# Gated cross-attention with a top-2 expert layer on one core: the prologue reordered, constant rows filled by two engines, weight loads in pairs, tiles aligned to 64 bytes

## The reference

```python
# attention: q from layernorm(x), k and v from ctx; 16 heads of 8
scores = einsum('bhqd,bhkd->bhqk', Q, K) / sqrt(8) + mask + window   # |i-j|<=32 or a global token (<16)
x = x + tanh(g_xattn) * (softmax(scores) @ V @ wo + bo)
# 8 experts, the best 2 for each token, F = 512
h = layernorm(x)
w, idx = top_k(softmax(h @ gate_w), 2); w = w / w.sum()
x = x + tanh(g_ffn) * sum_i w_i * (silu(h @ w1[i]) * (h @ w3[i])) @ w2[i]
```

## Time and profile before

| | us |
|---|---|
| median of 3 runs | 486.2 |
| lowest, highest | 484.93, 486.38 |
| profiled execution: span from the first to the last instruction | 458.1 |
| PE busy in the span | 407.4 (89%) |
| DVE, POOL, ACT busy | 290.9, 259.4, 239.6 |

### The profile page before, as it was taken

One profiled execution on the slowest core, in us unless ns is written; L12 is line 12 of the kernel. 1 busy time (PEld: TensorE's weight loads), 2 busy tenths in 40 slices (PEclk: granted clock), 3 DMA queues, 4 the chain that ended last, 5 costly groups with the idle time before them and its releaser, 6 DMA issues.

```text
span 458.1 us, 14422 instructions
## 1 busy us (share of the span) xinstructions
PE 407.4 (89%) x4547; PEld 360.1 (79%) x4548; DVE 290.9 (64%) x786; ACT 239.6 (52%) x564; POOL 259.4 (57%) x312
## 2 busy tenths in 40 slices
PE   2879979999999998997879899988999999999970
PEld 1647658877777776776669799888999999999960
DVE  3876798887888887889546368544444554554420
ACT  2758506667677675766666534233444444444430
POOL 5743554334654737473646568776666665655560
PEclk9989979999999999999999999999999999999995
DMA  7964557457766666485223233334444343333235
GB/s 215 279 123 94 96 96 185 90 105 113 170 147 136 152 134 161 106 216 169 65 69 75 45 52 48 54 67 61 69 70 58 44 54 46 46 47 40 24 29 189
DMA packets 74783, 46.24 MB, mean 101 GB/s; under 512 B 8608, under 2 KB 71490, under 8 KB 74562
## 3 DMA queue, kind: packets, MB, share of 16 engines
q1 hardware_dynamic: 59072, 34.84, 33.2%
q0 software_dynamic: 12272, 8.92, 14.9%
q10 hardware_dynamic: 3392, 1.88, 1.7%
HBM read 18.12 MB, written 14.20 MB: 71 GB/s over the span
## 4 chain that ended last, share of the span: by engine, by line
PE 62%; DMA 9%; issue 7%; DVE 6%; ACT 6%; POOL 4%; ACTq 2%; POOLq 1%; DVEq 0%
PE ps_scores L1612 20%; PE ps_max_scores L1620 10%; DMA sums_scratch<-yt,xg 8%; PE ps_values L897 7%; PE ps_max_scores L853 6%; PE ps_scores L883 5%; PE ps_scores L837 3%; PE ps_max_scores L837 2%; POOL expert_rows_scratch L1328 2%; PE ps_out L921 1%; ACT xn L474 1%; DVE rsplit L1119 1%; ACT w_all L464 1%; DVE qkf L558 1%; POOL sums_scratch L1733 1%
## 5 line engine op out<-in xcount | busy, mean ns | idle before, releaser
L1733 POOL DMA_INDIRECT sums_scratch<-yt,xg x71 | 115.9, 1633 | 66.9 <-DMA sums_scratch<-yt,xg 28.1
L1612 PE MATMUL ps_scores<-xgT,qs 128*128 128x128 f32 x1136 | 141.1, 278 | 5.1 <-ACT xgT L1658 3.8
L1612 PEld LDWEIGHTS ps_scores<-xgT,qs 128*128 128x128 f32 x1136 | 134.1, 194 | 7.1 <-ACT xgT L1658 4.5
L1699 DVE TENSOR_TENSOR qs<-qs,ps_scores 128x512 f32<-128x512 f32 x71 | 48.8, 688 | 88.4 <-PE ps_scores L1612 70.5
L1119 DVE TENSOR_REDUCE rsplit<-ps_max_scores 128x4 f32<-128x512 f32 x128 | 84.8, 685 | 15.0 <-PE ps_max_scores L837 11.2
L1328 POOL DMA_INDIRECT expert_rows_scratch<-xr,pos x64 | 66.4, 1037 | 25.6 <-issue 13.1
L1620 PE MATMUL ps_max_scores<-w_all,qs 128*128 x568 | 75.6, 276 | 2.8 <-ACT yt L1669 2.3
L1620 PEld LDWEIGHTS ps_max_scores<-w_all,qs 128*128 128x128 f32 x568 | 69.0, 192 | 3.8 <-issue 3.6
L1027 ACT ACTIVATE pT<-ps_scores 128x1024 f32<-128x1024 f32 x64 | 62.0, 1022 | 18.1 <-PE ps_scores L837 17.8
L1662 ACT ACTIVATE qs<-ps_scores 128x512 f32<-128x512 f32 x71 | 42.3, 596 | 30.3 <-PE ps_scores L1612 30.3
L1669 ACT ACTIVATE yt<-ps_max_scores,xg 128x128 f32<-128x128 f32 x71 | 26.1, 368 | 60.4 <-PE ps_max_scores L1620 40.4
(11 more groups left out here) (202 smaller groups left out, 527.8 us busy)
## 6 DMA issues: line engine op xcount, KB each, us to landing
qs<-w_all SPq DMA_DIRECT2D x96, 64.0 KB
ks<-w_all SPq DMA_DIRECT2D x96, 64.0 KB
w_all<-in_L_ffn_w_dram SPq DMA_DIRECT2D x24, 256.0 KB
xg<-expert_rows_scratch SPq DMA_DIRECT2D x71, 65.0 KB, 1.9
xs<-in_x_dram SPq DMA_DIRECT2D x4, 512.0 KB, 5.6
sums_scratch<-xs SPq DMA_DIRECT2D x8, 256.0 KB, 4.5
sums_scratch<-yt,xg POOLq DMA_INDIRECT x71, 3.3
expert_rows_scratch<-fill SPq DMA_DIRECT2D x16, 65.0 KB, 2.5
```

Source lines behind the costliest of these rows:

```text
L1612: ins = nc.tensor.matmul(bank[u % 2][:, c * P:(c + 1) * P], w13[:, u % 2, n, c * P:(c + 1) * P], xgT[:], start=True, stop=True)
L1699: nc.vector.tensor_tensor(hidT[:, u % 2], act_s[:, u % 2], ps_b[u % 2], ALU.mult).then_inc(hid_ready, 1)
L1733: pool.indirect_dma_start(out=z_d, out_offset=bass.IndirectOffsetOnAxis(ap=xg_u[:, u, X_IDX:X_IDX + 1], axis=0), in_=yt[:, u % YRING], in_ ...
```

## The change

- **Loads.** x comes in five chunks of 1, 1, 2, 2, 2 groups instead of four of two. `wo`, `bo`, `gate_w`, the mask, `bv` and the two gates are issued by SP instead of ACT, `wo` and the mask ahead of `fixed`. The biases have a semaphore of their own, so that the projection waits for three weights only.
- **ACT.** A one-element square root is executed right behind the weights' DMAs, which moves the load of its table there. Copy and normalise of the first groups change places; `std` 3 stands behind `copy_turned(3)`, `std` 4 behind `first_part(2)`.
- **PE.** Group 0 is projected before the router's four matmuls and group 1's turn; the turns of groups 1 and 2 stand between a group's q/k and v matmuls.
- **DVE.** Statistics of the last two chunks move behind `split` of groups 1 and 2.
- **Constant rows.** DVE fills `qs0`, POOL fills `ks0` in one instruction each; `qs1` and `ks1` are filled by DVE in four halves, one for each of groups 2 to 5 (`fix_second`). The 11 copies by SP are gone. The halves of group 1 wait for all four fills.
- **Weights.** No block of six; behind each half from group 2 on up to two pieces go, in order, of experts below the group's number.
- **Alignment.** Tiles whose size is an odd multiple of 32 bytes get 32 bytes of padding behind them.

```diff
+LINE = 64
         def sb(name, shape, dt=F32):
-            return stack.enter_context(nc.sbuf_tensor(name, shape, dt))
+            tile = stack.enter_context(nc.sbuf_tensor(name, shape, dt))
+            used = int(np.prod(shape[1:])) * (2 if dt == BF16 else 4)
+            if -used % LINE >= LINE // 2:
+                stack.enter_context(nc.sbuf_tensor(f"{name}_rest", [P, LINE // 8], F32))
+            return tile
...
-        XCH = 4
+        CHUNKS = (GB, GB, 2 * GB, 2 * GB, 2 * GB)
...
             load_x(0)
             load_ctx(0)
+            load_x(1)
             load_ctx(1)
-            load_x(1)
+            load_x(2)
+            sp.dma_start(mrow[:], mask_in).then_inc(mask_loaded, 16)
+            sp.dma_start(wo_x[:, 0:D], wo).then_inc(router_loaded, 16)
...
-            for side, (tile, rows) in enumerate(((qs, STAY_ROWS[0]), (ks, STAY_ROWS[1] + ((ROWS_M, ROWS_X),)))):
-                sp.wait_ge(fixed_ready, side + 1)
-                for lo, hi in rows:
-                    sp.dma_start(tile[1][lo:hi], tile[0][lo:hi]).then_inc(tile_copied, 16)
-
+            sp.wait_ge(fixed_ready, 1)
+            sp.wait_ge(keys_fixed, 1)
             sp.wait_ge(mpart_stored, 16)
             for g in range(2):
                 sp.wait_ge(parts_ready, g + 1)
                 if g == 1:
-                    sp.wait_ge(tile_copied, 16 * TILE_COPIES)
+                    sp.wait_ge(second_fixed, FIXES)
...
+        def fixed_rows(side, u, heads):
+
+            to = (qs, ks)[side][u][0:ROWS_X, heads].rearrange("p h (b s) -> p (h b) s", s=S)
+            return to, fixed[0:ROWS_X, side].unsqueeze(1).to_broadcast([ROWS_X, to.shape[1], S])
...
+            pool.wait_ge(fixed_loaded, 16 * 4)
+            keys, rows = fixed_rows(1, 0, slice(0, H))
+            pool.tensor_copy(keys, rows).then_inc(keys_fixed, 1)
...
+            last_part(0)
             pool.memset(wmask[:], 0.0).then_inc(pool_step, 1)
...
+            def fix_second(n):
+
+                nc.vector.tensor_copy(*fixed_rows(n // 2, 1, slice(n % 2 * (H // 2), (n % 2 + 1) * (H // 2))))\
+                    .then_inc(second_fixed, 1)
...
             for g in range(NG - 2):
                 split(g, g % 2)
                 bias_v(g)
-                if g < 2:
+                take_gates(g)
+                if 0 < g < 3:
+                    statistics(g + 2)
                     invert(g + 2)
-                if g == 0:
-                    statistics(3)
-                take_gates(g)
+                if g >= 2:
+                    fix_second(g - 2)
...
-            for e in range(2):
-                for n in range(3):
-                    load_weights(e, n)
+            pieces = [(e, n) for e in range(E) for n in range(3)]
             for g in range(2, NG):
...
-                    if g >= 3:
-                        for n in (range(0, 1), range(1, 3))[p]:
-                            load_weights(g - 1, n)
+                    for piece in range(2):
+                        if pieces[0][0] < g:
+                            load_weights(*pieces.pop(0))
```

More of the change, by code:

```diff
@@ L188, in build, with chunk, chunk_of @@
         idx_f = sb("idx_f", [P, 2, GB])
-        XCH = 4
-        x_loaded = [sem(f"x_loaded{i}") for i in range(XCH)]
+        CHUNKS = (GB, GB, 2 * GB, 2 * GB, 2 * GB)
+        assert sum(CHUNKS) == B
+        def chunk(i):
+            return slice(sum(CHUNKS[:i]), sum(CHUNKS[:i + 1]))
+        def chunk_of(g):
+            return 0 if g == 0 else 1 + g // 2
+        x_loaded = [sem(f"x_loaded{i}") for i in range(len(CHUNKS))]
         proj_loaded = sem("proj_loaded")
+        bias_loaded = sem("bias_loaded")
         by_dim_ready = sem("by_dim_ready")
@@ L509, in statistics @@
             def statistics(i):
-                n = B // XCH
+                at = range(B)[chunk(i)]
                 dve.wait_ge(x_loaded[i], 16)
-                for b in range(i * n, (i + 1) * n):
+                for b in at:
                     nc.vector.bn_stats(stats[:, b], xs[:, b]).then_inc(var_stats, 1)
-                dve.wait_ge(var_stats, (2 * i + 1) * n)
-                for b in range(i * n, (i + 1) * n):
+                dve.wait_ge(var_stats, at.start + at.stop)
+                for b in at:
@@ L586, in project_tensor, with turn @@
         def project_tensor(pe):
-            def turn(g, u, between=None):
+            def turn(g, u):
                 if not (isinstance(g, int) and g == 0):
@@ L636, in project_tensor, with second @@
             pe.wait_ge(ident_ready, 2)
-            turn(0, 0, turn_router)
-            turn(1, 1)
+            turn(0, 0)
             pe.wait_ge(proj_loaded, 16 * PROJ)
             pe.wait_ge(by_dim_ready, 2)
-            for g in range(NG - 2):
+            def second():
+                turn_router()
+                turn(1, 1)
+            project(0, 0, second)
+            project_gates(0, 0)
+            project(1, 1, lambda: turn(2, 0))
+            project_gates(1, 1)
+            turn(3, 1)
+            for g in range(2, NG - 2):
                 project(g, g % 2)
```

123 lines of the change are left out of this document (63 added, 60 removed).

## The result

| us | before | changed |
|---|---|---|
| median of 4 runs | 485.63 | 513.69 |
| lowest, highest | 484.93, 486.38 | 510.87, 515.93 |
| profiled execution: its own time | not given | 515.93 |
| its span | 458.1 | 514.2 |

The ratio is 1.0596, with a 95% interval of 1.0526 to 1.0665: 28.1 us more, where 13.3 were forecast and 505 was the end of the range.

What follows compares the result with a forecast made beforehand. PE's own work was taken to bound attention and experts, leaving only the prologue loose. Terms 3.7 + 0.3 + 5.7 + 3.6 = 13.3 us gave span 471.4 and, with 28.1 around it, 499.5 us; range 486.5 to 505.

Steps and rivals of the forecast that it cites:

- The start: Prologue: projection starts between 9.5 and 11, but POOL's copy holds DVE's `shift` until 23.4; group 1 ends 3.7 us later.
- Group 1 to 2: Prologue round between the ends of these groups' first parts: 9.3 us against 8.97 before, so +0.3.
- Group 2 to 3: Prologue: ACT waits for the last chunk's statistics, put behind group 2's split; 10.85 us against 5.17, so +5.7.
- Groups 3 to 6: Prologue: DVE's fills wait for POOL's third part, rounds become 5.6 us; split of group 6 17.0 us behind, +3.6.
- first softmax scores at 81.0: Start of attention: PE's first softmax scores move from 67.69 to 81.0, by the summed 13.3 us.
- Padding changes no count and no shape ... so I give it zero: Tile alignment: `w_all` reads run in the experts' window with PE full, so padding was put at zero.
- The rest of the span, 390.4 us, follows unchanged: Attention and experts: PE's own work is the bound, so everything after the first softmax scores keeps its length.
- PE waited on the halves of group 1: Attention: named as a sign of being wrong; forecast had these halves in place by 85, wanted at 86 and 96.
- The 28.1 us around the span, taken as fixed: Outside the profiled span: 28.1 us added to span 471.4 to give 499.5, assuming the profile was of a median run.
- At nothing: SP's queue: removing the 11 copies (15.8 us of queue) and splitting the block of six weight loads change nothing.
- the rivals: Four alternatives: POOL's copy not holding DVE (0.15), ACT setting the pace (0.15), no change (0.06), Slower still (0.07).
- Slower still: Rival, prologue: POOL copies at its two-input rate, 17.0 us; 8.3 us more, 507.8 in all; chance 0.07.

Runs made afterwards that it cites:

- after_scores_256_again: Repeat of after_scores_256 (changed kernel, padding kept, spacer putting score tiles on a multiple of 256 bytes) in the fifth session: 473.43 us, 1.0295 of the kernel before.
- after_old_layout: Changed kernel with every tile at its address of before (no padding, new small tile behind the others): 501.49 us, no ratio given.
- fifth session: Last session of experiments: changed kernel word for word (480.52 us) beside it with score tiles on a multiple of 256 bytes (473.43); kernel before 459.9.
- 485 session: A session in which the unchanged kernel before had a median near 485 us: 484.7 in the second, 486.4 in the third; the head's times (485.6) belong to one.
- 460 session: A session in which the unchanged kernel before had a median near 460 us: 460.1, 460.2 and 459.9 in the first, fourth and fifth.
- after_old_weights: Changed kernel with the weight loads in the order of before (block of six behind group 1's halves): 478.57 us, 1.0392 of the kernel before.
- after_fourth: Changed kernel word for word, timed again in the fifth session: 480.52 us, 1.0433 of the kernel before.
- after_scores_256: Changed kernel with its padding and a 128-byte spacer putting the score tiles on a multiple of 256 bytes again: 471.91 us, 1.0266 of the kernel before.
- before_scores_128: Kernel before with a 128-byte spacer ahead of the score tiles, which begin 128 bytes past a multiple of 256: 463.9 us, 1.007 of the kernel before.
- after_third: Changed kernel word for word, timed and profiled in the third session: 509.12 us, 1.0446 of the kernel before.
- before_third: Kernel before, word for word, timed and profiled again in the third session: 487.94 us, ratio 1.0039.

## Why the prediction was wrong

Step by step, in the prediction's own terms (the changed kernel's profile against the one of before):

- **The start**: projection at 11.08, forecast 9.5 to 11. Near enough. `shift` of the third chunk at 21.07, forecast 23.4, since POOL's copy starts at 11.70 and not 12.3 and takes 7.01 and not 8.7. Group 0's first part ends at 21.45, forecast 18: the root of the third chunk stands ahead of it and waits for the held tensor_scalar, which the prediction overlooked. Group 1 ends at 27.98: +2.2, forecast +3.7. Mechanism right, the copy mis-sized.
- **Group 1 to 2**: 37.62 - 27.98 = 9.6 us, +0.7, forecast +0.3.
- **Group 2 to 3**: 10.7 us, +5.5, forecast +5.7; ACT's wait for the last root is there, 5.33 us, and goes when the statistics move.
- **Groups 3 to 6**: split of group 6 at 64.48, 16.15 us behind; +2.7, forecast +3.6. The fills beside POOL's third part last 2.68, forecast 2.5.
- **Sum up to there** 11.2, forecast 13.3. The first softmax scores come at 81.58 all the same, because a term is missing that happens to be as large: from the split of group 6 they are 17.1 us away and were 14.4. The row maxima's DMA takes 7.57 us. With the score tiles on a multiple of 256 it is 78.5 - 63.96 = 14.5 us again (after_scores_256_again), and 14.9 in after_old_layout. So "first softmax scores at 81.0" was right by two errors that cancel.
- **"Padding changes no count and no shape ... so I give it zero"** is the step that failed. It looked at reads by engines and not at the DMAs that write into the moved tiles. The new small tile moved them too. Their address, 128 bytes past a multiple of 256, makes a packet 1.28 times as long and costs 6.3 to 7.1 us of the changed kernel's 20.7 in the fifth session. In a 485 session, like that of the result, single profiles give up to 12.8 in attention and 3.8 ahead of it. Half of the 12.8 is PE busy for longer, 163.9 us at a clock of 0.93 against 157.6 at 0.99.
- **"The rest of the span, 390.4 us, follows unchanged"** failed with it. PE was full in the one window that was read, 68 to 75, but this was not shown for the 160 us of the stage, where a DMA of 12 KB stands in each batch's path. The prediction had as a sign of being wrong that "PE waited on the halves of group 1"; PE waited on the row maxima's DMA, which the sum had nowhere.
- **The 28.1 us around the span, taken as fixed**, were wrong: 1.7 us lie there. The profile and the times came from different kinds of session, 25 us apart. By chance it put the forecast on the right base, but it hid that attention is 20 us longer in such a session, with PE idle for 25.2 us of the stage and not 11.4, so that the stage taken as full was not.
- **At nothing, SP's copies and the block of weights**: right within what the runs can tell in a 460 session. after_old_weights and after_fourth, each against before, have intervals that overlap (1.0358 to 1.0425 and 1.0361 to 1.0505), and attention in after_scores_256 and after_scores_256_again takes 162.6 and 159.8 us, against 160.8.

With the score tiles on their multiple of 256 the forecast holds in 460 sessions: 11.7 and 13.6 us over before in two of them, where 13.3 was forecast. In the one 485 session with old addresses it is 15.1, of runs that scatter too much for an interval. Of the rivals none came true; the copy on POOL did hold DVE for its whole length. "Slower still" had a time near the measured one, 507.8, for a reason that the 7.01 us of the copy rules out.

Open are three things: what lengthens attention by 20 us in a 485 session, from about 115 us on; how the 28 us of that session divide exactly, since no pair on both addresses was timed in one with a usable interval; and what the order of weights is worth there. Where it was measured well, the address costs 6.3 to 7.1 us and the rest of the change 11.7 to 13.6; the 7 us between 20.7 and 28.1 have no run that settles them.

## What to carry to other kernels

When a change moves tiles in memory, look up which DMAs write into them and in what pieces: 512-byte rows into a tile on a multiple of 256 bytes took 53 ns and 68 ns with the tile 128 past one, and "aligned to 64" was a step down from an alignment that was there by luck. Before a later stage is called unchanged, list the small transfers in its loop with the room each has, since here slower bulk traffic in another queue went with their landing late, and PE waited for them. Compare the span of the profile with the timed runs, too: 28 us between them was no overhead but another kind of session.

## What was not expected of the hardware

- A POOL copy, 124x8192 in bfloat16, took 7.01 us, and the same copy on DVE 2.28. Beside it a DVE tensor_scalar on 128x8 in float32, with one input, took 6.73 us and not 0.17. So it isn't only instructions with two SBUF inputs that are held, as the prediction had it.
- The kernel before took 460 us in three sessions and 485 in two, both on the chip of the third and the fifth, and its profiles of the two kinds have an equal prologue (67.7 us) and a stage of attention of 160.8 and 181.1 us.
- A block of six loads of 256 KB, each time directly behind the two halves of group 1, held SP's queue for 5.54 us in before, 7.30 with the score tiles 128 past a multiple of 256 (before_scores_128), and 10.89 in after_old_weights, where attention had already begun.
- In after_third the granted clock fell to 0.50 several times in attention, once for 6.8 us after 6.8 us in which PE was busy for 4.46; in before_third it is 1.00 in the whole stage.
